# Finer waits, one register for the bound, and output image by image in a conv, mixture-of-experts and attention kernel on one core

## The reference

```
slot = where(pos < cap, expert * cap + pos, E * cap)       # E * cap: dropped
eb = zeros((E * cap + 1, C)).at[slot].set(x_token)          # scatter
h = gelu(eb @ W1 + b1);  y = h @ W2 + b2                    # per expert
moe = sum over 2 picks of y[slot] * gate                    # gather, gate 0 if dropped
x = input + norm + layer_scale * moe
x_h = x.mean(3) + x[..., :w//2].mean(3) + x[..., :w//4].mean(3)     # x_w alike
a_h, a_w = sigmoid(wh @ hswish(w1 @ [x_h, x_w])), ...
out = silu(bn(conv3x3(x * a_w * a_h)))
```

## Time and profile before

| | |
|---|---|
| median of 3 runs | 6482.2 us (6470.43 to 6500.45) |
| the profiled execution | 6459.45 us, of which the trace spans 6457.7 us |
| convolution, norm, routing | 0 to 1470 us |
| experts | 1470 to 4022 us, the scatters of POOL until 3857 |
| output | 4022 to 6457.7 us, the gathers of POOL until 6247 |
| first tile on PE | 1631.64 us |
| POOL clears `padded` (L1050) | 11.3 us, from 4022; first gather 4034.3 |
| busy | PE 75%, POOL 57%, VectorE 37%, ACT 23% |

### The profile page before, as it was taken

How to read it: one execution, slowest core, us unless ns; L and a number is a source line. 1 busy time by engine, 2 the same in 40 slices (tenths; PEclk the granted TensorE clock), 3 DMA queues, 4 the chain that set the end, 5 groups by cost and what they waited for, 6 DMA issues and landing times. The chain is left out here.

```text
span 6457.7 us, 68952 instructions
## 1 busy us (share of the span) xinstructions
PE 4826.4 (75%) x20564; PEld 2703.6 (42%) x20564; DVE 2372.3 (37%) x4527; ACT 1459.3 (23%) x3608; POOL 3676.8 (57%) x3625
## 2 busy tenths in 40 slices
PE   9999998110677879797797679067877767867869
PEld 4556668100344445444454344034444333433434
DVE  0012237991122222222222122355555455545542
ACT  2233346410222323232232223001000001000001
POOL 0000000007878787787878770778777777877750
PEclk9999999555888989898898889579998888889989
DMA  8887779822333333232232222334445799999970
GB/s 170 186 185 193 194 187 274 288 77 85 88 102 103 109 98 102 84 93 84 84 99 80 78 70 74 116 104 116 129 117 117 104 110 108 117 110 120 117 68 30
DMA packets 840382, 770.16 MB, mean 119 GB/s; under 512 B 594480, under 2 KB 668172, under 8 KB 836050
## 3 DMA queue, kind: packets, MB, share of 16 engines
q1 hardware_dynamic: 666322, 466.30, 26.6%
q0 software_dynamic: 109312, 198.40, 23.4%
q10 hardware_dynamic: 64512, 102.79, 4.6%
HBM read 440.11 MB, written 385.75 MB: 128 GB/s over the span
## 5 line engine op out<-in xcount | busy, mean ns | idle before, releaser
L1075 POOL DMA_INDIRECT y_ring<-ye,index_o x1568 | 1720.7, 1097 | 461.9 <-issue 461.6
L759 POOL DMA_INDIRECT xe<-chunk,index x1568 | 1539.4, 982 | 477.3 <-issue 476.4
L1108 PE MATMUL cp<-padded,taps_o 128*128 128x448 f32 x4032 | 1636.2, 564 | 195.6 <-DVE padded L1294 102.4
L1108 PEld LDWEIGHTS cp<-padded,taps_o 128*128 128x128 f32 x4032 | 787.4, 199 | 972.9 <-issue 829.5
L888 ACT ACTIVATE hid<-hid_ps,b_cols 128x448 f32<-128x448 f32 x1120 | 709.4, 633 | 1663.1 <-PE hid_ps L842 1565.1
L850 PE MATMUL y_ps<-hid,w_sb 128*128 128x448 f32 x2240 | 916.3, 553 | 0.4 <-DVE yt L913 0.4
L842 PE MATMUL hid_ps<-xt,w_sb 128*128 128x448 f32 x2240 | 890.9, 541 | 1.5 <-DVE xt L907 1.5
L907 DVE COPY xt<-xt_ps 128x448 f32<-128x448 f32 x280 | 175.0, 625 | 1283.1 <-PE xt_ps L833 1280.5
L471 POOL MEMSET zeros<- 98x512 f32 x1 | 0.5, 524 | 1108.4 <-POOLq L105 1108.4
L1239 DVE SCALAR_TENSOR_TENSOR z<-y_ring,gates,z 128x128 f32<-128x128 f32 x1568 | 432.6, 347 | 523.6 <-DMA y_ring<-ye,index_o 500.8
L1172 ACT ACTIVATE outb<-cp,shift,s 128x448 f32<-128x448 f32 x224 | 162.1, 724 | 1999.5 <-PE cp L1108 1150.0
(11 more groups left out here) (189 smaller groups left out, 3542.6 us busy)
## 6 DMA issues: line engine op xcount, KB each, us to landing
xe<-zeros SPq DMA_DIRECT2D x16, 3920.0 KB
rows_in<-xe SPq DMA_DIRECT2D x280, 224.0 KB, 2.6
ye<-rows_out SPq DMA_DIRECT2D x280, 224.0 KB
xin<-in_x_dram SPq DMA_DIRECT2D x256, 196.0 KB
conv<-rows ACTq DMA_DIRECT2D x256, 196.0 KB
pix<-conv SPq DMA_DIRECT2D x224, 224.0 KB, 5.1
xn<-hat SPq DMA_DIRECT2D x112, 448.0 KB, 4.4
chunk<-xn POOLq DMA_DIRECT2D x112, 448.0 KB, 4.0
```

What stands on the lines that cost most here:

```text
L759: pool.indirect_dma_start(out=xe[:, :], out_offset=bass.IndirectOffsetOnAxis(ap=index[ch][:, c, j:j + 1], axis=0), in_=chunk[ch][:, j * C: ...
L1075: pool.indirect_dma_start(out=y[ch][c][:, j * C:(j + 1) * C], out_offset=None, in_=ye[:, :], in_offset=bass.IndirectOffsetOnAxis(ap=index[ ...
L1108: last = pe.matmul(cp[i % 2][:, 0:HB * W], taps[:, t, :], padded[b][:, img, hb * HB + kh:hb * HB + kh + HB, kw:kw + W], start=(t == 0), st ...
```

## The change

- **The bound in a register.** `limit = pool.to_reg(...)` is made once in each of the two phases, and all 3136 indirect DMAs use it. The MOVEs ahead of them are gone.
- **Tiles wait for chunks.** `needed` counts chunks (1 to 112) and not pairs. POOL raises `chunks_scattered` for chunk n-1 after it has issued chunk n. Two waits of POOL on older scatters are gone. The table is worked out by tile on partitions, with smaller VectorE operations, and SP copies it to one partition.
- **Drops skipped.** The bound of the gathers is DROP - 1, so that dropped picks fetch nothing; ye has no row DROP. POOL clears each slot of `y_ring` once, in the first pair. The margins of `padded` are cleared by VectorE and no longer by POOL.
- **Gather limit.** POOL gathers chunk n only once PE has transposed chunk n-3.
- **Output by image.** Attention is made twice for each pair, for the first image after chunk 3 and for the second after chunk 6, on arrays of half the size. The convolution of an image starts right after its own attention. The sums of the next chunk are placed ahead of the scaling. There are 4 buffers `outb`.

```diff
@@ route_phase
+            do(dve.tensor_scalar(short[:], run[:, :, 0:GR - 1], tile_end[:, 0:1], None, ALU.is_lt))
+            do(dve.tensor_reduce(fewer[:], short[:], AX_X, ALU.add))
+            dve.tensor_scalar(needed_by_tile[:], fewer[:], 1.0, None, ALU.add).then_inc(needed_set, 1)
-            do(dve.tensor_tensor(short[:], by_pair.unsqueeze(1).to_broadcast([128, TILES, E, PR - 1]),
-                                 tile_end[:].unsqueeze(2).unsqueeze(3).to_broadcast([128, TILES, E, PR - 1]), ALU.is_lt))
-            do(dve.tensor_reduce(fewer[:], short[:], AX_X, ALU.add))
...
@@ expert_phase
+            limit = pool.to_reg(DROP - 1)
...
-                    if not (first and ch < 2):
-                        pool.wait_ge(scattered[ahead], ahead_pair * PER_PAIR)
-                    if not first or ch == NCHK - 1:
-                        pool.wait_ge(scattered[(ch + 1) % NCHK], (g + (ch + 1) // NCHK) * PER_PAIR)
...
-                                bounds_check=DROP - 1, oob_is_err=False).then_inc(scattered[ch], 16)
+                                bounds_check=limit, oob_is_err=False).then_inc(scattered[ch], 16)
+                    if n:
+                        pool.wait_ge(scattered[(ch - 1) % NCHK], (g + (1 if ch else 0)) * PER_PAIR)
+                        pool.sem_inc(chunks_scattered, 1)
                     rest(n)
-                    if ch == 0 and not first:
-                        for c in range(NCHK):
-                            pool.wait_ge(scattered[c], g * PER_PAIR)
-                        pool.sem_inc(pairs_scattered, 1)
...
@@ output_phase, POOL
+            limit = pool.to_reg(s["DROP"] - 1)
...
+                    if n >= 3:
+                        pool.wait_ge(tp_done, n - 2)
...
+                    if first:
+                        pool.memset(y_ring[:, ch * 2 * CC:(ch + 1) * 2 * CC], 0.0).then_inc(cleared, 1)
+                        pool.wait_ge(cleared, ch + 1)
...
-                                bounds_check=s["DROP"], oob_is_err=False).then_inc(y_in[ch], 16)
+                                bounds_check=limit, oob_is_err=False).then_inc(y_in[ch], 16)
...
@@ output_phase, PE
+                    for _ in range(BEHIND[ch]):
+                        bank(img, i)
                         i += 1
+                    if ch in LAST_CHUNK:
+                        bank(img, i)
+                        bank(img, i + 1)
+                        at = g * 2 + img
+                        pe.wait_ge(pooled_ready, at + 1)
...
```

More of the change, by code:

```diff
@@ L506, in _ @@
             pe.wait_ge(consts_set, 2)
+            pe.matmul(sums[:, 0, 0:1], below[:], tile_rows[:], start=True, stop=True).then_inc(tiles_counted, 1)
             for r in range(SEARCH_STEPS):
@@ L981, in output_phase @@
         weigh = sb("weigh", [C, A])
-        outb = [sb(f"outb{i}", [C, HB * W]) for i in range(2)]
+        outb = [sb(f"outb{i}", [C, HB * W]) for i in range(OUTS)]
         tp = [ctx.enter_context(nc.psum_tensor(f"tp{b}", [128, 1024], F32)) for b in range(2)]
@@ L1000, in output_phase @@
         conv_done, conv_read = sem("conv_o_done"), sem("conv_o_read")
-        out_done = [sem(f"out_done{i}") for i in range(2)]
+        out_done = [sem(f"out_done{i}") for i in range(OUTS)]
         block = ctx.enter_context(nc.Block())
@@ L1113, in body, with bank @@
             def body(g, b, first, last_pair, first_prev=False):
-                i = 0
+                def bank(img, i):
+                    if img == 1:
+                        conv_bank(g, b, i, first)
+                    elif not first:
+                        conv_bank(g - 1, 1 - b, IB + i, first_prev)
+                img, i = 0, 0
                 for ch in range(NCHK):
-                    if not first:
-                        for _ in range(BEFORE[ch]):
-                            conv_bank(g - 1, 1 - b, i, first_prev)
-                            i += 1
                     nn, q = g * NCHK + ch, (b + ch) % 2
@@ L1153, in _ @@
             body(PR - 1, 1, False, True, PR == 2)
-            for i in range(NB):
-                conv_bank(PR - 1, 1, i, False)
+            for i in range(IB):
+                conv_bank(PR - 1, 1, IB + i, False)
         @block.scalar
@@ L1197, in _ @@
             body(PR - 1, 1, False, True, PR == 2)
-            for i in range(NB):
+            for i in range(IB, NB):
                 conv_out(PR - 1, 1, i, False)
-            for o in range(2):
-                act.wait_ge(out_done[o], 16 * (PR * NB // 2))
+            for o in range(OUTS):
+                act.wait_ge(out_done[o], 16 * (PR * NB // OUTS))
         @block.vector
         def _(dve):
+            for b in range(2):
+                last = dve.memset(padded[b][:], 0.0)
+            last.then_inc(margins_set, 1)
             for t in range(9):
@@ L1253, in add, with attend @@
                                          ALU.add, ALU.add).then_inc(added, 1)
-            def body(g, b, first, last_pair):
-                if first:
-                    sums(g, 0)
-                for ch in range(NCHK):
-                    if ch + 1 < NCHK:
-                        sums(g, ch + 1)
-                    elif not last_pair:
-                        sums(g + 1, 0)
-                    add(g, b, ch)
-                dve.wait_ge(added, g * NCHK + NCHK)
-                steps.round(g)
-                dve.tensor_reduce(quarter[:, 0].rearrange("c n h q -> c (n h q)"),
-                                  summed[b][:].rearrange("c (a r) -> c a r", r=W // 4), AX_X, ALU.add)
-                for img in range(2):
-                    view = summed[b][:, img * HW:(img + 1) * HW].rearrange("c (q r w) -> c w q r", q=4, w=W)
-                    last = dve.tensor_reduce(quarter[:, 1, img], view, AX_X, ALU.add)
-                steps.done(last)
+            def attend(g, b, img, last):
+                at = g * 2 + img
+                image = summed[b][:, img * HW:(img + 1) * HW]
+                steps.round(at)
+                dve.tensor_reduce(quarter[:, 0].rearrange("c h q -> c (h q)"),
+                                  image.rearrange("c (a r) -> c a r", r=W // 4), AX_X, ALU.add)
+                steps.done(dve.tensor_reduce(quarter[:, 1], image.rearrange("c (q r w) -> c w q r", q=4, w=W), AX_X, ALU.add))
@@ L1278, in body @@
[L1278 removed]
+                steps.done(dve.scalar_tensor_tensor(pool_t[:], quarter[:, :, :, 1], full + halfw, pool_t[:], ALU.mult, ALU.add))
+                dve.scalar_tensor_tensor(pooled[:].rearrange("c (d h) -> c d h", d=2), quarter[:, :, :, 0],
                                          full + halfw + quart, pool_t[:], ALU.mult, ALU.add).then_inc(pooled_ready, 1)
[L1281 removed]
+                dve.wait_ge(att1_done, at + 1)
```

136 lines of the change are left out of this document (70 added, 66 removed).

## The result

The changed kernel takes 6245.8 us (median of 4 runs, 6244.1 to 6249.3) where the kernel before took 6476.3 beside it (6426.9 to 6500.5): a ratio of 0.965 (95% interval 0.962 to 0.969). It is faster, but by 3.5% and not by 17%; 5400 and the whole range were wrong, and rival A (6230) is what happened. The profiled span is 6243.3 us.

What follows compares the result with a forecast made beforehand. POOL's own pace was taken to set both phases, then PE finishes. Output starting at 3495 plus 1883 us of output gave a 5378 span, 5380 profiled, times 1.0035: 5400 us, range 5300 to 5750.

Steps and rivals of the forecast that it cites:

- rival A: Ahead of POOL's indirect DMAs: the 0.30 us gap is the DMA's own and stays without MOVEs; 6230 us, chance 0.13.
- the part on the gap: Ahead of POOL's indirect DMAs: removing the MOVE saves the whole 0.30 us gap each; bounds 0.03 and 0.30.
- Output 1883 us by the prediction: Output phase: 1 us setup, 118 first pair, 15 x 111 = 1665, tail 97, barrier 2; before 2436.
- the "-0.3" a chunk for skipped rows: POOL's gathers in the output phase: skipped rows save 0.024 us on each of 14 gathers a chunk.
- The factor 1.0035: Whole kernel: median of the runs, 6482.2, over the profiled execution, 6459.45; applied to the 5380 forecast.
- Routing: VectorE's work before the first scatter: smaller operations save 10 us (bounds 12 and 5), first scatter at 1466.
- The tail of the experts: PE after POOL's last scatter: 8 tiles of the last round wait for the last chunk, before 22 to 24.
- The tail of the output: From the last gather to the end: 7 banks left after the last scaling, about 97 us in all.
- A pair on PE alone: Output phase: PE needs 103 us a pair plus two waits of 2 us for scaled images, 107.
- The limit of three chunks: POOL's gathers waiting on PE's transposes: the limit doesn't bind, by 3 us.
- The stretched gathers: Output phase: four gathers a pair, beside VectorE's scaling, last 3.16 us instead of 1.00 and stay so.
- The first tile on PE: Expert phase: PE starts at 1553, five chunks of 17.06 us and 2 us after 1466; before 1631.64.

## Why the prediction was wrong

**The step that failed** is in the part on the gap: "I take 0.30, because the rows without a MOVE, a DMA row among them, have no gap at all." The bounds were 0.03 and 0.30, and the saving was 0 (477.3 and 460.4 us of "issue" with the MOVEs and without). The rows without a gap were plain loads and memsets, so they differed from the others in two ways, no MOVE and not indirect, and I put all of it on the first. The start of the MOVE at the end of the DMA ahead is right as a reading, but the 0.30 us are there with or without it, so what fills them doesn't wait for the MOVE. The rule of the Trainium skill (Advanced Engine Details and Errata, Sequencer and Instruction Queues) that the prediction weighed and set aside had the outcome right: removal gives nothing. By rows 4 the MOVE still doesn't run under the DMA ahead.

**What hangs on it.** 14 x 0.30 us a chunk: scatters over at 3377 by the prediction, at 3849.7 in the trace, so the output phase starts 423 us later (3495 to 3917.7). Output 1883 us by the prediction, 2325.6 in the trace, 443 more. 423 + 443 = 866, all of the miss (6243.3 - 5378 = 865).

**Rival A's own terms.** Scatters over at 3847 (3849.7), output phase at 3919 (3917.7), both good to 3 us. Output 2285 (2325.6): 41 us short, of which 38 are the "-0.3" a chunk for skipped rows (0.024 x 14 x 112). The median gather was 1004 ns before and after; the 980 ns of a scatter are the scatter's. So that term should have been 0, and A would have had 6244 for the span, where 6243.3 was measured. That nearness is in part luck: set-up and gathers took 11 us more than A has, and the end 8 less. The factor 1.0035 from the profiled execution to the median was 1.0004 in the changed kernel; with it A would have read 6266.

**Right in their size.** These terms held. Routing: the first scatter came 7.7 us earlier (forecast 10, bounds 5 and 12). The tail of the experts: 8 tiles for 22 to 24, 97 us in the trace and 91 when undone alone. The tail of the output: 97 by the prediction, 90.8 in the trace, since the last chunk was transposed 7 us after the last gather and not 13. A pair on PE alone: 107 to 111 by the prediction, 108.7 once POOL was out of the way. The limit of three chunks: POOL waited for L1130 not once. The stretched gathers stay, and they were 140 us that the prediction passed over as given. The 4 buffers: no wait of ACT for a store is left among the large ones.

**Right by luck.** The first tile on PE came at 1558.5, and 1553 was forecast. But the forecast had five chunks of 17.06 us in it; with the real 21.26 the same working gives 1576. The tile came 4.3 chunks after the first scatter.

**Left open.** How the 44 us of the backlog divide among the skipped drops, the four buffers and the order isn't shown. What PE waits for on the slower chip isn't shown, nor whether the limit of three chunks, or its absence, does anything elsewhere. What the 0.30 us are spent on inside POOL no row shows; one indirect DMA for more than 128 rows, which would have fewer of them, wasn't tried.

## What to carry to other kernels

A gap ahead of an operation belongs to whatever all the gapped operations have in common, and when two things go together in every row, the trace can't choose: price both ends, and give the lower end the chance it deserves. When one engine issues back to back with nobody to wait for, only its own time counts: 3136 indirect DMAs of 1.28 us and more, a pause of 295 us and 140 us of stretched gathers counted for more than bytes or landing times. Fine waits and a finer output stage are worth what PE still has to do after that engine's last instruction, here about 91 and 101 us, and nothing in the middle. And follow the chain that ended last up to the end: here the engine that never waits was at work to 6247, but from 5624 on a second chain, the stores, was the later one.

## What the runs showed of the hardware

- An indirect DMA of 128 rows of 512 bytes on POOL costs 0.98 us (scatter) or 1.00 us (gather), and 0.30 us ahead of it behind another DMA; after a memset it was 0.28, after a small TENSOR_TENSOR 0.16. With 6 in 10 rows skipped it costs the same (mean 1107 ns, and 1102 with all rows fetched). A plain one of the same size, on rows that lie together, costs 0.53 us with no gap.
- A VectorE operation of 3.43 us on two tensors in SBUF makes the indirect DMA beside it last 3.0 to 4.2 us, most often 3.16. With one of the two in PSUM the operation lasts 3.42 us and the DMA 1.00.
- One row that 6 in 10 picks fetch raised the DMA share from 0.24 to 0.98 (5200 to 6140 us) at 77 and 110 GB/s. The share was no sign of a bound in the kernel with four store buffers: it cost 9 us of 6250. In the kernel before, with the row and two buffers, the stores took 15 to 34 us each from 5624 us on and had become the chain that ended last.
- One and the same program took 6430 to 6480 us on some chips and 7420 on another. The four kernels traced on that one have PE pausing inside rows of matmuls (140.8 us under "issue" in L1110 with the weights in PSUM, where the changed kernel has none).
